# Two attention layers and two expert layers on one core: the next chunk's gating, one block or nine pieces

## What is computed

```
x = hidden.reshape(-1, 256)                        # 2048 tokens
logits = (x @ wt.T + repeat(g @ wg.T)) / 2         # 8 experts
scores = softmax(logits)
topk_w, topk_idx = top_k(scores, 2)
topk_w = topk_w / (topk_w.sum(-1) + 1e-20)
h_e = leaky(x @ w_gate[e]) * (x @ w_up[e])         # 256 -> 128, slope 0.01
y = sum over the two chosen e of topk_w * (h_e @ w_down[e])
p = leaky(x @ sw_gate) * (x @ sw_up) @ sw_down     # shared, 256 -> 256 -> 256
return y + p                                       # added to x by the caller
```

## Time and profile before

| | us |
|---|---|
| median of 3 runs | 1737.34 |
| lowest and highest of them | 1736.25, 1737.54 |
| profiled execution, its own time | 1732.54 |
| span of the profiled execution | 1730.6 |
| PE busy | 1470.3 (85%) |
| DVE busy | 1410.4 (81%) |
| ACT busy | 1210.2 (70%) |
| POOL busy | 751.0 (43%) |

### The profile page before, as it was taken

The page is one execution under the profiler, slowest core; times in us unless marked ns, Lnnn a source line. Parts: engine busy times, 40 slices in busy tenths (PEclk is TensorE's granted clock), DMA queues, the critical chain, the costliest instruction groups (busy, mean ns, idle before and its releaser), DMA issues.

```text
span 1730.6 us, 46424 instructions
## 1 busy us (share of the span) xinstructions
PE 1470.3 (85%) x16377; PEld 1081.0 (62%) x16377; DVE 1410.4 (81%) x3651; ACT 1210.2 (70%) x3064; POOL 751.0 (43%) x1412
## 2 busy tenths in 40 slices
PE   2467778888889999977888888999999799999998
PEld 1245556666677777766666666777777555555555
DVE  4557778888889999977788888999999687777777
ACT  1268778888889899978888888989999432332232
POOL 5557776443434334366554232223222365522222
PEclk9779999999999999989999999999999899999999
DMA  4002122111211223012121212221223000000000
GB/s 138 7 24 62 51 62 75 57 62 69 75 58 67 87 99 99 33 44 62 51 81 52 85 63 75 75 81 62 82 99 99 1 25 19 1 1 1 13 13 25
DMA packets 50440, 96.70 MB, mean 56 GB/s; under 512 B 3332, under 2 KB 27028, under 8 KB 50212
## 3 DMA queue, kind: packets, MB, share of 16 engines
q1 hardware_dynamic: 45504, 90.27, 15.8%
q10 hardware_dynamic: 4708, 3.45, 0.7%
HBM read 91.54 MB, written 2.17 MB: 54 GB/s over the span
## 4 chain that ended last, share of the span: by engine, by line
PE 42%; DVE 21%; ACT 14%; issue 11%; POOL 3%; DMA 1%; DVEq 0%; ACTq 0%; SPq 0%; POOLq 0%
PE tp L1312 7%; DVE p_lo L964 7%; ACT p_hi L722 6%; DVE biased L880 5%; PE sc L1203 3%; PE sc L1086 3%; PE sc L1087 3%; PE sc L1088 3%; ACT q_b L651 3%; PE sc L1204 3%; ACT probs L630 3%; PE op L1086 2%; PE aux L1086 2%; PE tp L1086 2%; PE aux L1088 2%
## 5 line engine op out<-in xcount | busy, mean ns | idle before, releaser
L964 DVE TENSOR_TENSOR p_lo<-tp,p_hi 128x512 f16<-128x512 f32 (+3 forms) x768 | 416.6, 554 | 121.3 <-ACT p_hi L722 114.3
L880 DVE CUSTOM_DVE_ANT_0 biased<-sc,bias,neg_null 128x256 f32<-128x256 f32 (+7 forms) x512 | 411.0, 803 | 2.7 <-issue 0.8
L630 ACT ACTIVATE probs<-biased,neg_max 128x256 f32<-128x256 f32 (+7 forms) x512 | 395.7, 773 | 14.2 <-DVE neg_max L880 12.7
L1312 PE MATMUL tp<-ident,probs 128*128 128x128 f32 x2304 | 388.7, 278 | 17.7 <-DVE p_lo L964 15.5
L722 ACT ACTIVATE p_hi<-tp 128x512 f16<-128x512 f32 (+3 forms) x768 | 368.9, 491 | 43.6 <-PE tp L1312 33.5
L1086 PE MATMUL op<-v_s,p_hi 128*128 128x64 f16 x2304 | 284.9, 194 | 54.4 <-DVE p_lo L964 35.9
L1203 PE MATMUL sc<-k_a,q_a 128*128 128x512 f16 (+3 forms) x768 | 254.2, 331 | 66.2 <-DVE neg_max L880 59.3
L1312 PEld LDWEIGHTS tp<-ident,probs 128*128 128x128 f32 x2304 | 267.9, 142 | 52.9 <-issue 37.9
L1088 PE MATMUL op<-v_s,p_lo 128*128 128x64 f16 x2304 | 284.0, 194 | 0.0
L1087 PE MATMUL op<-v_s,p_hi 128*128 128x64 f16 x2304 | 283.9, 194 | 0.0
L1086 PEld LDWEIGHTS op<-v_s,p_hi 128*128 128x128 f16 x2304 | 216.0, 99 | 85.5 <-DVE p_lo L964 62.1
(11 more groups left out here) (257 smaller groups left out, 3611.4 us busy)
## 6 DMA issues: line engine op xcount, KB each, us to landing
bias<-rel_table SPq DMA_DIRECT2D x4, 2048.0 KB, 8.5
bias<-in_fside_16xSxS SPq DMA_DIRECT2D x4, 2048.0 KB, 7.9
bias<-rel_table SPq DMA_DIRECT2D x4, 1792.0 KB, 7.9
bias<-in_fside_16xSxS SPq DMA_DIRECT2D x4, 1792.0 KB, 7.1
bias<-rel_table SPq DMA_DIRECT2D x4, 1536.0 KB, 7.3
bias<-in_fside_16xSxS SPq DMA_DIRECT2D x4, 1536.0 KB, 6.7
bias<-rel_table SPq DMA_DIRECT2D x4, 1280.0 KB, 5.6
bias<-in_fside_16xSxS SPq DMA_DIRECT2D x4, 1280.0 KB, 6.3
```

Of the source, the lines that this page charges most:

```text
L630: ac.activation(probs[:, i % 2, 0:w], biased[:, i % 2, 0:w], ACT.Exp, bias=neg_max[:, u % 2, i % HU:i % HU + 1], scale=-1.0, accum_out=row ...
L880: ve.tensor_tensor_reduce(out=biased[:, i % 2, 0:w], in0=sc[i % 2][:, 0:w], in1=bias[:, g % 2, i % HU, 0:w], scale=-1.0, scalar=neg_null[: ...
L964: ve.tensor_tensor(p_lo[:, gi % 4, 0:nb * P], tp[gi % 2][:, 0:nb * P], p_hi[:, gi % 4, 0:nb * P], ALU.subtract).then_inc(s["p_lo"], 1)
L1312: last = te.transpose(tp[gi % 2][:, jj * P:(jj + 1) * P], probs[:, n % 2, (j0 + jj) * P:(j0 + jj + 1) * P], ident[:, :])
```

## The change

The work that prepares the next chunk is kept, operation for operation. Its places in the step loop are changed. `x_lo` is cut in two and `gate_pick` in six pieces (`gate_scores`, `gate_first` and `gate_drop` twice each, `gate_weights`), and with `gate_shift` each stands at a step of its own:

| step | before | after |
|---|---|---|
| 1 | | PE `x_t`, ACT `x_hi`, DVE `x_lo(0)` |
| 2 | | DVE `x_lo(1)` |
| 3 | | PE `logits`, DVE `gate_shift` |
| 4 | PE `x_t`, ACT `x_hi`, DVE `x_lo` | ACT `gate_exp`, DVE `gate_scores` |
| 5 | | DVE `gate_first(0)` |
| 6 | PE `logits`, DVE `gate_shift`, ACT `gate_exp` | DVE `gate_drop(0)` |
| 7 | DVE `gate_pick` | DVE `gate_first(1)` |
| 8 | | DVE `gate_drop(1)` |
| 9 | | DVE `gate_weights` |

The last operation of each of the first five of the six pieces keeps its `link`, the wait for its own completion; the last operation of `gate_weights` has none, as before. Waits on other engines are the same ones. The core of the diff:

```diff
@@ ScalarE
+                if cn + 1 < 2 * CHUNKS and e == 1:
+                    x_hi(cn + 1)
                 if cn + 1 < 2 * CHUNKS and e == 4:
-                    x_hi(cn + 1)
-                if cn + 1 < 2 * CHUNKS and e == 6:
                     gate_exp(cn + 1)
@@ VectorE
-            def gate_pick(cn):
+            def gate_scores(cn):
 
                 dve.wait_ge(f["exp"], cn + 1)
...
+            def gate_first(r):
+
+                left = gl[2] if r == 0 else gl[4]
+                link(ve.reduce_max(gm[2 + r][:, :], left[:, :, :], AX))
+                link(ve.tensor_tensor(gl[3][:, :, :], left[:, :, :], over_e(gm[2 + r]), ALU.is_equal))
+                link(ve.tensor_tensor(gl[3][:, :, :], gl[3][:, :, :],
+                                      place[:, :].unsqueeze(1).to_broadcast([P, CHUNK, E]), ALU.mult))
+
+            def gate_drop(r):
+
+                left = gl[2] if r == 0 else gl[4]
+                link(ve.reduce_max(gm[4][:, :], gl[3][:, :, :], AX))
+                link(ve.tensor_tensor(gl[3][:, :, :], gl[3][:, :, :], over_e(gm[4]), ALU.is_equal))
+
+                link(ve.scalar_tensor_tensor(gl[4 + r][:, :, :], gl[3][:, :, :], -4.0, left[:, :, :],
+                                             ALU.mult, ALU.add))
...
                 if cn + 1 < 2 * CHUNKS:
+                    if e == 1:
+                        x_lo(cn + 1, 0)
+                    if e == 2:
+                        x_lo(cn + 1, 1)
+                    if e == 3:
+                        gate_shift(cn + 1)
                     if e == 4:
-                        x_lo(cn + 1)
+                        gate_scores(cn + 1)
+                    if e == 5:
+                        gate_first(0)
                     if e == 6:
-                        gate_shift(cn + 1)
+                        gate_drop(0)
                     if e == 7:
-                        gate_pick(cn + 1)
+                        gate_first(1)
+                    if e == 8:
+                        gate_drop(1)
+                    if e == 9:
+                        gate_weights(cn + 1)
@@ TensorE
                 if cn + 1 < 2 * CHUNKS:
-                    if e == 4:
+                    if e == 1:
                         x_t(cn + 1)
-                    if e == 6:
+                    if e == 3:
                         logits(cn + 1)
```

More of the change, by code:

```diff
@@ L991, in _, with x_lo @@
                                          ALU.subtract, ALU.mult).then_inc(s["y_n"], 1)
[L994 to L998, removed]
+            def x_lo(cn, kc):
+                bank = (op, aux)[kc]
+                dve.wait_ge(f["xt_hi"], KC * cn + kc + 1)
+                ve.tensor_tensor(mx_lo[:, cn % 2, kc, :], bank[:, :], mx_hi[:, cn % 2, kc, :], ALU.subtract)\
+                    .then_inc(f["xt_lo"], 1)
             def over_e(t_):
@@ L1012, in gate_shift @@
                 ve.tensor_tensor(gl[0][:, :, :], gl[2][:, :, :], over_e(gm[0]), ALU.subtract).then_inc(f["shifted"], 1)
-            def gate_pick(cn):
+            def gate_scores(cn):
                 dve.wait_ge(f["exp"], cn + 1)
-                sc_ = gl[2]
                 link(ve.reduce_sum(gm[0][:, :], gl[1][:, :, :], AX))
                 link(ve.reciprocal(gm[1][:, :], gm[0][:, :]))
[L1020 to L1032, removed]
@@ new lines, in gate_scores @@
+                link(ve.tensor_tensor(gl[2][:, :, :], gl[1][:, :, :], over_e(gm[1]), ALU.mult))
+            def gate_first(r):
[4 more added lines that the diff above has]
+                                      place[:, :].unsqueeze(1).to_broadcast([P, CHUNK, E]), ALU.mult))
@@ L1033, in gate_pick, with gate_weights @@
+            def gate_drop(r):
[4 more added lines that the diff above has]
+                                             ALU.mult, ALU.add))
+            def gate_weights(cn):
                 link(ve.scalar_tensor_tensor(gm[4][:, :], gm[2][:, :], 1e-20, gm[3][:, :], ALU.add, ALU.add))
@@ L1034, in gate_pick @@
                 link(ve.reciprocal(gm[5][:, :], gm[4][:, :]))
-                link(ve.tensor_scalar(gl[3][:, :, :], left[:, :, :], 0.0, 1.0 / WS, ALU.is_lt, ALU.mult))
-                link(ve.tensor_tensor(gl[3][:, :, :], gl[3][:, :, :], sc_[:, :, :], ALU.mult))
+                link(ve.tensor_scalar(gl[3][:, :, :], gl[5][:, :, :], 0.0, 1.0 / WS, ALU.is_lt, ALU.mult))
+                link(ve.tensor_tensor(gl[3][:, :, :], gl[3][:, :, :], gl[2][:, :, :], ALU.mult))
                 ve.tensor_tensor(comb[:, cn % 2, :, :], gl[3][:, :, :], over_e(gm[5]), ALU.mult).then_inc(f["comb"], 1)
@@ L1055, in _ @@
             dve.wait_ge(setup["place"], E)
-            x_lo(0)
+            x_lo(0, 0)
+            x_lo(0, 1)
             gate_shift(0)
-            gate_pick(0)
+            gate_scores(0)
+            gate_first(0)
+            gate_drop(0)
+            gate_first(1)
+            gate_drop(1)
+            gate_weights(0)
             for en in range(2 * CHUNKS * EB + 2):
```

## The result

| | before | after |
|---|---|---|
| median, us | 1737.44 (4 runs, 1736.25 to 1737.63) | 1706.26 (4 runs, 1705.49 to 1706.77) |
| profiled execution, us | 1732.54 | 1705.99 |
| its span | 1730.6 | 1704.2 |
| transposes of chunk 0 (first `x_t`) to the end of the span | 1370.32 to 1730.6, 360.28 | 1368.67 to 1704.2, 335.53 |

The account below looks back on a forecast made before the run. PE was taken to bound the kernel. From the median of 1737.34 us, 25.4 were taken off (25.6 of stalls and half clock, 0.2 back for POOL), giving 1711.9 us; range 1706.5 to 1718.5.

Parts of the forecast that it names:

- PE sets the pace, an undisturbed chunk takes 40.48 us: Expert part: ten steps of 3.90 us, transposes 0.88 and logits 0.60 on PE make 40.48 us.
- Seven stalls from one long stretch on DVE, 19.3 us: `down` waits for `y_evict` behind the uncut gate in chunks 0 to 6; 3 x 2.97 + 4 x 2.6 us won.
- Four drops of the clock, 6.3 us: PE at half clock behind the stalls of chunks 1, 3, 4, 5, about 1.5 us each; 6.3 us won.
- the lower part of my case: A median run may have drops behind all seven stalls: 4.5 us more won, 1707.4 us.
- Six pieces fit: Gate pieces on DVE, steps 4 to 9: 0.67 us each, the last 0.96, against 0.92 spare; PE sees none.
- The margin of 0.74 us: Between DVE's fourth eviction and the second half of `down`: DVE can fall 0.74 us behind before PE notices.
- the 0.2 us of waits that I had set for POOL: POOL running beside the gate pieces in chunks 0 to 2: 0.2 us added, between nothing and 0.8 us.
- Moves at steps 1 to 3 at nothing: `x_t`, `x_hi`, `x_lo` at steps 1 and 2, `gate_shift` at step 3: DVE's spare time covers them, no cost.
- The clock that stays: Rival: half clock comes from PE's long full load, so only 19.3 us are won, 1718.0 us; chance 0.05.
- The one without effect: Rival: DVE's debt is carried, not worked off; seven stalls return at step 9 at full size, 1737.3 us; chance 0.04.
- the slower one: Rival: 28 short stalls of 0.3 us, each with 1.5 us of half clock, 1762.1 us; chance 0.03.
- POOL holding DVE: Rival: every piece in chunks 0 to 2 waits 1.2 us for POOL; these win nothing, 1722.3 us; chance 0.05.

Follow-up runs that it names:

- filler kernel: The kernel before with 12 matmuls of 512 columns, read by nothing, in front of `down` at step 9 of chunks 0 to 6; 1726.61 us, ratio 0.9949.
- moved block: The changed kernel with the gate behind the shift uncut at step 4, both `x_lo` at step 1; 1734.34 us, ratio 0.9994 to the kernel before.

## Why the prediction was right, and where not

**PE sets the pace, an undisturbed chunk takes 40.48 us.** Right to the hundredth: 40.48 in all periods of the changed kernel read above.

**Seven stalls from one long stretch on DVE, 19.3 us.** Right. The filler kernel has them without drops, 2.98 and 2.6 us in a period, and the moved block brings all of them back.

**Four drops of the clock, 6.3 us.** The mechanism was right. The size was right for the profiled execution, 6.15 us against the filler's profile, and probably too small for a median run. I took the number of drops from that one execution, faster than all the runs shown beside it, and carried it over to the median; a second profile has five, and the filler wins 8.9 us in the median (6.3 to 11.3). I had put up to 4.5 us more into the lower part of my case and not into the forecast, although the profiled execution lay 4.8 us under the median and three more drops at 1.5 us would have explained nearly all of that. By ratios, the 29.5 us are 8.9 of drops and 20.6 of stalls and the rest, against my 6.3 and 19.3; by the profiles, 6.15 and 18.6. The 4 us by which the forecast fell short lie between the profiled execution and the median. More drops in a usual run are the likeliest cause, which is inferred and not counted.

**Six pieces fit.** Right in the outcome, less so in the numbers: 0.83 and 1.42 us in chunk 0 in place of 0.67 and 0.96. I had bounded the last piece at 1.33. The margin of 0.74 us took it, and the 0.2 us of waits that I had set for POOL didn't come. The 20 operations take 5.6 us in sum there, below the 6 that I had named as a sign of being wrong.

**Moves at steps 1 to 3 at nothing.** Right: no wait of PE beside them. In chunk 0, PE's wait of 0.34 us before the third `gate_up` is gone, but there PE runs 12 matmuls of the first `gate_up` at half clock where it was six, which takes most of the 0.85 us by which the profiled difference of the changed part is 24.75 us and not 25.6. That is not the change's doing: the second profile of the kernel before has 12 at half clock too, no wait of 0.34, and reaches the next transposes 0.7 us later than the first.

**The rivals.** The clock that stays is refuted by the filler. The one without effect and the slower one: no sign of either; chunks with 0.5 to 1.65 us of short stalls had no drop. POOL holding DVE: I had argued it away with 0.37 us on 20 operations, and this argument was weak. Of those operations in chunk 0, twelve ran after POOL's last one had ended at 1410.57, and the others met only what was left of `h_lo` or short operations. The rows had the hold already: the 0.40 us operation at 1408.94 ended at 1409.34, POOL's of the earlier trace rows at 1409.31. Its price was right only for the place that the change happened to choose, and that part was luck.

## What to carry to other kernels

When one engine sets the pace, a long side task on another costs only what its longest uncut stretch has above one step's idle time plus the margin to the pacing engine. Work out both from one quiet step; here cutting below them won all, and moving alone won nothing. Take the number of clock drops from more than one execution, or from the gap between the profiled execution and the median. And look at what the third engine is doing at the very spot where a piece goes in, since 0.8 us may decide over 25.

## What the runs showed of the hardware

A DVE operation with two SBUF inputs that starts while a POOL operation runs waits for its end: 1.03 and 1.17 us in place of 0.19, ending 0.04 to 0.06 us behind POOL's 1.16 us operation. A reciprocal with one input that lay wholly inside POOL's operation (1463.27, beside POOL's 1463.12 to 1464.27) took its usual 0.18. The Trainium skill, page SBUF — State Buffer, section "SBUF: two separate sides", says that a VectorE instruction with two SBUF inputs and a GpSimd one that reads SBUF share a pair of ports, which the first to start holds for its whole instruction while the other waits, and the measurement agrees. A 32-column `tensor_scalar`, which has one tensor input, was held too (0.83 us in place of 0.18, in the kernel with the pieces inside `y_evict`):

```profile
1463.48 0.83 DVE L1043 TENSOR_SCALAR gl<-gl 128x32 f32<-128x32 f32 x1
```

PE waits of 2.4 to 2.8 us brought half of the 2.4 GHz clock four times in one execution and five times in another of the same program, out of seven; excesses of 0.5 to 1.65 us per chunk, in single waits of up to 1.07 us, brought none, and neither did the wait of 1.70 us in the last steps of the kernel before and the changed one. Matmuls whose result nobody reads, put into the wait, kept the clock up and were worth 8.9 us (6.3 to 11.3) by themselves. What decides between a wait with a drop and one without was not found.
